# An attentional factorization machine on one core: two fills read from the given table, transposes four rounds later

## The chip, the cores and the metric

The kernel runs on one core of one Trainium2 chip. The metric is the device time of one execution in microseconds. Three executions of the kernel before took 846.13, 851.7 and 852.37 us, median 851.7.

## The reference

For 2048 samples with 32 fields each, rows of an embedding table (12500 x 64) are gathered; only the core of it is shown:

```python
V = emb_v[x]                                     # 32 x 2048 x 64
iu, ju = np.triu_indices(32, k=1)                # 496 pairs of fields
VV = V[iu] * V[ju]
hid = relu(einsum('pbk,kh->pbh', VV, at_w) + at_b)   # 64 -> 64
score = einsum('pbh,ho->pbo', hid, at_h)
pooled = sum(VV * score, axis=0)
logit = pooled @ p + w0 + sum(w1[x], axis=0)     # w1: 12500 x 1
prob = sigmoid(logit)
```

All of it is float32. `x` is drawn below 100000, and the reference clamps it to the table.

## The kernel before, in words

**Fills.** The batch is cut into 32 fills (`FILLS`) of 64 samples, 16 from each quarter of the batch, in two groups g of 32. A fill needs 16 indirect gathers of 128 rows each (line 276): tile (g, m) and half, into one of two buffers `rows[t % 2]`. TensorE transposes the gathered rows (`turn`, eight 128x128 transposes) into a slot of the PSUM buffer `Z`; ScalarE copies them to `V` (`keep_v`, line 424).

**The joint table.** The linear weight `w1[x]` is needed beside the embedding. So the head of the kernel loads the whole table in four pieces and a tail of 212 rows, joins it with `w1` into rows of 66 numbers (w1, embedding, w1; lines 327 to 332 on VectorE, 454 on ScalarE), and stores them as `table` in DRAM (`store_piece`, SP lines 243 to 246 and ScalarE line 456). From then on a gather brings 65 numbers from `table` with `joint_idx`. Only the first group of fill 0 is gathered from the given `emb_v`, and its w1 values are gathered at the end (line 302, 8 gathers). GpSimd waits for `table_stored` before the second group of fill 0.

**Rounds.** A fill has 16 rounds, (step s, group g). VectorE makes the products of pairs `X` (line 409, two instructions a round, four step slots), TensorE multiplies by `at_w` (`hidden`, line 549, into one of three `Z` slots), ScalarE applies bias and ReLU (line 489, into `H`), and TensorE reduces by `at_h` (`scores`, line 564), two steps at a time: after round 3 those of steps 6 and 7 of the fill before, after rounds 7, 11 and 15 those of steps 0 to 5 (`SCORED_AFTER`). I call hidden rounds h0 to h15 and the four score blocks s67, s01, s23, s45.

**Grams.** The pooled sum is taken through the pairwise products weighted by p: ScalarE makes two halves of `pV` (`keep_pv`, line 435), TensorE multiplies `pV` by `V` (`grams`, line 579, 128 small matmuls into `SG`), VectorE masks them (`mask_gram`, line 370), and once all eight steps are scored it multiplies and sums (`weigh` line 378, `sum_pairs` line 384). `grams(t)` must be masked before the first score of fill t is added to the same PSUM tile.

**Order.** Each engine's order is written out by hand; fill 0 is written separately, then a loop with two fills a turn (`over_fills`), then the last fill. In the kernel before, the transposes of fill t+1 are put before h8 of fill t (`TURN_BEFORE = 8`), `keep_v` in ScalarE's round 8, the halves of `pV` in rounds 10 and 14, `keep_w1` (copy of the w1 columns, line 443) in round 12, and the grams of fill t+1 after s45 of fill t. VectorE masks at round 8, weighs at 10, sums at 12. GpSimd's gathers of fill t are paced in four groups of four by the `scored` and `z_ready` counts of fills t-3 and t-2 (`GROUP_AFTER`).

**Head and end.** SP issues the index loads, two table pieces, the tail and nine small loads; ScalarE two pieces and w1. TensorE begins with `first_turn(0)` only after `consts_ready` and all nine small loads, then `keep_busy`, h0 to h3 of group 0, `first_turn(1)`, and the rest. At the end `linear_term` (line 622) waits for the late w1 gathers.

## Time and profile before

| | us |
|---|---|
| median of three executions | 851.7 (846.13 to 852.37) |
| the profiled execution | 846.66 |
| its span | 844.6 |
| TensorE matmul busy | 785.1 (93%) |
| VectorE busy | 701.3 (83%) |
| ScalarE busy | 648.1 (77%) |
| GpSimd busy | 549.0 (65%) |
| mean granted TensorE clock | 0.988 |

The span is the profiled execution from its first to its last instruction; 2.1 us lie around it. In the page a time behind a bar, "idle before", is what the engine stood still ahead of these instructions. In a timeline the bracket at the end of a row gives that idle time and who ended it. "issue" is a wait for which the profile shows no other engine. SPq and ACTq are the DMA issues of SyncE and ScalarE.

### The profile page before, as it was taken

What the parts mean: (1) busy time and instruction counts of PE and PEld (TensorE: products, weight loads), DVE (VectorE), ACT (ScalarE), POOL (GpSimd) and SP (SyncE); (2) the same over time, 40 slices, a digit from 0 to 9 for tenths busy, and PEclk for the clock granted to TensorE, in tenths of its full rate; (3) what the DMA queues carried; (4) which work ended last, traced back from release to release, by engine and by line L of the source; (5) the groups of instructions that cost most, each with busy time, mean ns of one, the idle gap of its engine ahead of it and who ended that gap; (6) DMA issues with size and microseconds to landing.
All of it is one profiled execution on the core that took longest, in us unless ns stands there. A gap on an engine that the chain in (4) does not pass through costs nothing.

```text
span 844.6 us, 30455 instructions
## 1 busy us (share of the span) xinstructions
PE 785.1 (93%) x12600; PEld 336.8 (40%) x12600; DVE 701.3 (83%) x1181; ACT 648.1 (77%) x679; POOL 549.0 (65%) x530
## 2 busy tenths in 40 slices
PE   0368799999999999999999999999999999999998
PEld 0123344444434444444344444434444444344443
DVE  3367788889988888899888889998888899888883
ACT  2256577878888788888878888887878788887885
POOL 4377776666677666666776666667766666767500
PEclk9979899999999999999999999999999999999999
DMA  7458887532424436333233436352322436323100
GB/s 238 107 26 26 25 25 26 22 22 22 22 23 23 21 21 23 21 22 23 22 23 22 22 21 22 22 25 20 23 22 21 22 21 23 24 20 23 9 1 2
DMA packets 19138, 24.20 MB, mean 29 GB/s; under 512 B 9705, under 2 KB 9774, under 8 KB 19118
## 3 DMA queue, kind: packets, MB, share of 16 engines
q0 software_dynamic: 16640, 17.07, 39.5%
q1 hardware_dynamic: 1703, 3.61, 1.1%
q10 hardware_dynamic: 774, 3.25, 1.0%
q8 instruction: 13, 0.21, 0.1%
q14 instruction: 8, 0.06, 0.0%
HBM read 20.59 MB, written 3.31 MB: 28 GB/s over the span
## 4 chain that ended last, share of the span: by engine, by line
PE 83%; POOL 4%; issue 4%; DVE 3%; DMA 3%; SPq 2%; ACT 0%; DVEq 0%; POOLq 0%
PE Z L549 50%; PE SG L564 26%; POOL rows L276 4%; PE SG L579 4%; PE Z L513 4%; DVE X L409 3%; DMA table<-joined 1%; DMA rows<-table,joint_idx 1%; SPq L236 1%; PE Z L634 0%; SPq L237 0%; SPq L229 0%; SPq L239 0%; SPq L238 0%; DVE part L384 0%
## 5 line engine op out<-in xcount | busy, mean ns | idle before, releaser
L276 POOL DMA_INDIRECT rows<-table,joint_idx x504 | 531.0, 1054 | 233.9 <-issue 144.9
L409 DVE TENSOR_TENSOR X<-V 128x992 f32<-128x992 f32 (+15 forms) x1024 | 635.9, 692 | 40.9 <-PE Z L549 22.0
L489 ACT ACTIVATE H<-Z,bias 128x1024 f32<-128x1024 f32 x512 | 536.6, 1118 | 112.5 <-PE Z L549 109.2
L549 PE MATMUL Z<-X,w_sb 64*64 64x512 f32 x4096 | 473.6, 598 | 9.2 <-issue 5.1
L549 PEld LDWEIGHTS Z<-X,w_sb 64*64 64x64 f32 x4096 | 153.0, 133 | 242.4 <-issue 237.4
L564 PE MATMUL SG<-H,score_w 128*32 128x496 f32 (+15 forms) x4096 | 248.4, 382 | 0.0
L564 PEld LDWEIGHTS SG<-H,score_w 128*32 128x32 f32 x4096 | 109.4, 110 | 204.0 <-issue 109.5
L435 ACT ACTIVATE pV<-V,pmask 128x1024 f32<-128x1024 f32 x64 | 81.0, 1269 | 0.1
L378 DVE TENSOR_TENSOR prod<-SG,gram 128x496 f32<-128x496 f32 x32 | 21.6, 674 | 67.5 <-PE SG L564 67.5
L424 ACT COPY V<-Z 128x1024 f32<-128x1024 f32 x31 | 31.4, 1014 | 43.0 <-PE Z L513 43.0
L579 PE MATMUL SG<-V,pV 128*32 128x32 f32 x4096 | 43.7, 198 | 3.2 <-ACT pV L435 1.6
L579 PEld LDWEIGHTS SG<-V,pV 128*32 128x32 f32 x4096 | 43.1, 109 | 7.1 <-issue 3.8
L513 PE MATMUL Z<-ident,rows 128*128 128x128 f32 x248 | 34.7, 284 | 5.8 <-DMA rows<-table,joint_idx 5.8
L525 PE MATMUL SG<-ident,rows 128*128 128x128 f32 x8 | 2.2, 428 | 38.7 <-DMA rows<-in_L_rec_emb_v_dram,idx 29.9
L513 PEld LDWEIGHTS Z<-ident,rows 128*128 128x128 f32 x248 | 27.3, 143 | 8.7 <-DMA rows<-table,joint_idx 5.0
L370 DVE TENSOR_TENSOR gram<-SG,upper 128x496 f32<-128x496 f32 x32 | 21.6, 675 | 9.8 <-PE SG L579 8.2
L384 DVE TENSOR_REDUCE part<-prod 128x496 f32 (+1 forms) x32 | 21.1, 660 | 0.0
L525 PEld LDWEIGHTS SG<-ident,rows 128*128 128x128 f32 x8 | 1.4, 216 | 39.5 <-issue 29.9
L276 POOL DMA_INDIRECT rows<-in_L_rec_emb_v_dram,idx x8 | 9.3, 1168 | 10.4 <-DVE idx L317 8.3
L358 DVE COPY score_w<-hcol 64x1 f32<-64x1 f32 x32 | 2.2, 150 | 10.3 <-DMA w_sb<-in_L_rec_w_dram 10.3
L443 ACT COPY w_all<-rows 128x8 f32 (+2 forms) x64 | 10.4, 227 | 0.0
L463 ACT COPY V<-SG 128x512 f32<-128x512 f32 x2 | 1.2, 587 | 12.1 <-PE SG L525 12.1
(42 smaller groups left out, 31.9 us busy)
## 6 DMA issues: line engine op xcount, KB each, us to landing
rows<-table,joint_idx POOLq DMA_INDIRECT x504, 3.7
table<-joined ACTq DMA_DIRECT2D x2, 792.0 KB
table<-joined SPq DMA_DIRECT2D x2, 792.0 KB
raw<-in_L_rec_emb_v_dram ACTq DMA_DIRECT2D x2, 768.0 KB, 6.7
raw<-in_L_rec_emb_v_dram SPq DMA_DIRECT2D x2, 768.0 KB, 9.1
idx_raw<-in_r_x_dram SPq DMA_DIRECT2D x4, 64.0 KB, 5.9
rows<-in_L_rec_emb_v_dram,idx POOLq DMA_INDIRECT x8, 6.6
w_all<-in_L_rec_w_dram,idx POOLq DMA_INDIRECT x8
```

The source lines that it names most:

```text
L276: pool.indirect_dma_start(out=rows[t % 2][:, g * FILL_M + m, half, c0:c1], out_offset=None, in_=source, in_offset=bass.IndirectOffsetOnAxi ...
L370: nc.vector.tensor_tensor(gram[parity][:, :, 1:FIELDS], SG[parity][:, :, 1:FIELDS], upper[:, 1:FIELDS].unsqueeze(1).to_broadcast(shape), A ...
L378: nc.vector.tensor_tensor(prod[:, :, 1:FIELDS], SG[parity][:, :, 1:FIELDS], gram[parity][:, :, 1:FIELDS], ALU.mult).then_inc(prod_ready, 1)
L384: nc.vector.tensor_reduce(part[:, bass.ds(t * GROUP, GROUP)], prod[:, :, 1:FIELDS], AX.X, ALU.add).then_inc(part_ready, 1)
L409: last_one = nc.vector.tensor_tensor(xo, vj, vi.unsqueeze(3).to_broadcast(shape), ALU.mult)
L424: nc.scalar.copy(V[parity][:, :, :], Z[:, TURN_SLOT, :, :].rearrange("p g (b f) -> p (g b) f", f=FIELDS)).then_inc(v_ready, 1)
L435: nc.scalar.activation(pV[:, :, half, :, :], V[parity][:, :, :].rearrange("p b (i c) -> p b c i", c=2), ACT.Copy, scale=pmask[:, half:half ...
L489: nc.scalar.activation(H[:, s % H_SLOTS, :, COLS * g:COLS * g + COLS], Z[:, z_slot(r), :, :], ACT.Relu, bias=bias[:, 0:1]).then_inc(hid_re ...
L513: last = nc.tensor.transpose(Z[:, TURN_SLOT, g, 128 * m:128 * m + 128], embs[:, g * FILL_M + m, 1:1 + 2 * EMB], ident[:, :])
L549: done = nc.tensor.matmul(Z[64 * par:64 * par + 64, z_slot(r), half, :], w_sb[k, :], X[k, s % X_SLOTS, par, COLS * g:COLS * g + COLS], sta ...
L564: last = nc.tensor.matmul(SG[parity][at:at + 32, :, j0:FIELDS], score_w[:, slot, :], hid.rearrange("p (b j) -> p b j", j=nj), start=(s == ...
L579: last = nc.tensor.matmul(SG[parity][at:at + 32, b, :], pV[:, g * GROUP + b, half, :, :].rearrange("p c i -> p (c i)"), V[parity][:, g * G ...
```

## The change

1. Fills 0 and 1 (`PLAIN_FILLS = 2`) are gathered wholly from `emb_v` with the plain indices; the 32 w1 gathers that replace their w1 columns come at the end. `keep_w1` of fills 0 and 1 and the two memsets of the w1 columns go.
2. All four joined pieces and the tail are stored by SP, after the 16 gathers of fill 0 have landed. GpSimd waits for the table only before fill 2.
3. The index loads are split, two on SP and two on ScalarE's queue, where they are first; w1 comes ahead of the pieces there, w1's tail moves to SP, and its join (two copies) from VectorE to ScalarE.
4. `first_turn(0)` comes before the wait for the constants, and `keep_busy` makes four matmuls instead of eight.
5. The transposes of fill t+1 move from before h8 to before h12, with `keep_v`; `keep_w1` to round 14; the halves of `pV(t)` to rounds 0 and 2 of fill t itself, and the grams of fill t behind s67, after h3 of fill t. VectorE masks at 10, weighs at 11, sums at 13. The transposes of fill 1 keep their own slot.
6. The gathers of fill t are paced later: from two more scored steps (line 267) and from z_ready 6, 10 and 13 instead of 3, 7 and 10.

The declarations of two semaphores are left out below.

```diff
--- before.py
+++ after.py
@@ -43,7 +43,9 @@
 ORDER = [(s, g) for s in range(STEPS) for g in range(2)]
 FIRST_ORDER = [(s, g) for g in range(2) for s in range(STEPS // 2)] + ORDER[ROUNDS // 2:]
 
-TURN_BEFORE = 8
+TURN_BEFORE = 12
+PV_BEFORE = (0, 2)
+MASKED_BEFORE, WEIGHED_BEFORE, SUMMED_BEFORE = 10, 11, 13
 SCORED_AFTER = {3: (-1, (6, 7)), 7: (0, (0, 1)), 11: (0, (2, 3)), 15: (0, (4, 5))}
 LAST_STEPS = (6, 7)
 
@@ -55,9 +57,10 @@
 PIECES = 4
 PIECE = RUN // PIECES
 MAIN = 128 * RUN
+PLAIN_FILLS = 2
 TAIL_RUN = 4
 TAIL = (VOCAB - MAIN) // TAIL_RUN
-GROUP_AFTER = (0, 3, 7, 10)
+GROUP_AFTER = (0, 6, 10, 13)
 
 
 def segments(s):
@@ -71,7 +74,7 @@
     return (r if r < TURN_BEFORE else r + 1) % Z_SLOTS
 
 
-TURN_SLOT = TURN_BEFORE % Z_SLOTS
+TURN_SLOT, FIRST_TURN_SLOT = TURN_BEFORE % Z_SLOTS, Z_SLOTS - 1
 
 
 def z_before(r):
@@ -222,28 +225,33 @@
         def store_piece(eng, k):
             eng.dma_start(piece(table, k), joined[:, k * PIECE:(k + 1) * PIECE, :]).then_inc(table_stored, 16)
 
+        def load_idx(eng, q):
+            eng.dma_start(idx_raw[q * FIELDS:(q + 1) * FIELDS, :], r_x[:, q * NB:(q + 1) * NB]).then_inc(idx_loaded, 16)
+
         @block.sync
         def _(sp):
 
-            for q in range(QUARTERS):
-                sp.dma_start(idx_raw[q * FIELDS:(q + 1) * FIELDS, :],
-                             r_x[:, q * NB:(q + 1) * NB]).then_inc(idx_loaded, 16)
+            for q in range(QUARTERS // 2):
+                load_idx(sp, q)
             for k in range(PIECES // 2):
                 load_piece(sp, k)
             sp.dma_start(tail[:, :, 1:1 + EMB], last_rows(emb_v)).then_inc(tail_loaded, 16)
+            sp.dma_start(tail_w1[:, :], w1[MAIN:VOCAB, :].rearrange("(p r) o -> p (r o)", r=TAIL_RUN)).then_inc(tail_loaded, 16)
             for half in range(2):
                 lo, hi = half * 64, half * 64 + 64
-                sp.dma_start(pcol[lo:hi, :], p).then_inc(small_loaded, 16)
+                sp.dma_start(w_sb[lo:hi, :], at_w).then_inc(small_loaded, 16)
                 sp.dma_start(bias[lo:hi, :], at_b.rearrange("(h o) -> h o", o=1)).then_inc(small_loaded, 16)
                 sp.dma_start(hcol[lo:hi, :], at_h).then_inc(small_loaded, 16)
-                sp.dma_start(w_sb[lo:hi, :], at_w).then_inc(small_loaded, 16)
+                sp.dma_start(pcol[lo:hi, :], p).then_inc(small_loaded, 16)
             sp.dma_start(w0_sb[:, :], w0.to_broadcast([QUARTERS, 1])).then_inc(small_loaded, 16)
-            sp.wait_ge(w1_joined, 4)
-            sp.wait_ge(tail_loaded, 16)
-            sp.dma_start(last_rows(table), tail[:, :, :]).then_inc(table_stored, 16)
-            for k in range(PIECES // 2):
+            for g in range(2):
+                sp.wait_ge(first_rows[g], 16 * GATHERS // 2)
+            sp.wait_ge(w1_joined, 2)
+            for k in range(PIECES):
                 sp.wait_ge(rows_joined[k], 1)
                 store_piece(sp, k)
+            sp.wait_ge(tail_joined, 2)
+            sp.dma_start(last_rows(table), tail[:, :, :]).then_inc(table_stored, 16)
             sp.wait_ge(y_ready, 1)
             sp.dma_start(out.rearrange("(q a m) o -> a q (m o)", q=QUARTERS, a=QUARTERS), y_sb[:, :, :]).then_inc(y_stored, 16)
             sp.wait_ge(y_stored, 16)
@@ -259,16 +267,16 @@
 
             flat = table.rearrange("v (k o) -> (v k) o", o=1)
 
-            def gather(t, groups=(0, 1), paced=False):
-
-                for g in groups:
+            def gather(t, paced=False):
+
+                joint = t >= PLAIN_FILLS
+                source, at_rows = (flat, joint_idx) if joint else (emb_v, idx)
+                for g in range(2):
                     for m in range(FILL_M):
                         if paced and g == 0 and m == 0:
-                            pool.wait_ge(scored, STEPS * (t - 3) + LAST_STEPS[0] - 1)
+                            pool.wait_ge(scored, STEPS * (t - 3) + LAST_STEPS[0] + 1)
                         elif paced and m % 2 == 0:
                             pool.wait_ge(z_ready, ROUNDS * (t - 2) + GROUP_AFTER[2 * g + m // 2])
-                        joint = t > 0 or g > 0
-                        source, at_rows = (flat, joint_idx) if joint else (emb_v, idx)
                         for half in range(2):
                             col = (2 * half + g) * NM + t * FILL_M + m
                             c0, c1 = (0, ROW) if joint else (EMB_AT[half], EMB_AT[half] + EMB)
@@ -278,28 +286,24 @@
                                                     in_offset=bass.IndirectOffsetOnAxis(ap=at_rows[:, col:col + 1], axis=0)
                                                     ).then_inc(arrived, 16)
 
-            for half in range(2):
-                nc.gpsimd.memset(rows[0][:, 0:FILL_M, half, W1_AT[half]], 0.0).then_inc(w1_cleared, 1)
             pool.wait_ge(idx_ready, 1)
-            gather(0, groups=(0,))
+            gather(0)
+            pool.wait_ge(idx_ready, 2)
+            gather(1)
             pool.wait_ge(idx_ready, 4)
             pool.wait_ge(table_stored, 16 * (PIECES + 1))
-            gather(0, groups=(1,))
-            gather(1)
             pool.wait_ge(first_turned, 2)
-            pool.wait_ge(w1_kept, 2)
             gather(2)
             pool.wait_ge(rows_turned, 1)
-            pool.wait_ge(w1_kept, 4)
             gather(3)
             for t in range(4, FILLS):
                 pool.wait_ge(rows_turned, t - 2)
-                pool.wait_ge(w1_kept, 2 * (t - 1))
+                pool.wait_ge(w1_kept, 2 * (t - 3))
                 gather(t, paced=True)
-            for half in range(2):
-                for n in range(FILL_M):
-                    at = bass.IndirectOffsetOnAxis(ap=idx[:, 2 * half * NM + n:2 * half * NM + n + 1], axis=0)
-                    pool.indirect_dma_start(out=w1_all[:, 2 * half, n:n + 1], out_offset=None, in_=w1, in_offset=at
+            for Q in range(QUARTERS):
+                for n in range(PLAIN_FILLS * FILL_M):
+                    at = bass.IndirectOffsetOnAxis(ap=idx[:, Q * NM + n:Q * NM + n + 1], axis=0)
+                    pool.indirect_dma_start(out=w1_all[:, Q, n:n + 1], out_offset=None, in_=w1, in_offset=at
                                             ).then_inc(w1_first, 16)
 
         @block.vector
@@ -322,10 +326,9 @@
                                         ).then_inc(idx_ready, 1)
 
 
-            dve.wait_ge(w1_loaded, 32)
+            dve.wait_ge(w1_loaded, 16)
             for c in (0, 1 + EMB):
                 nc.vector.tensor_copy(joined[:, :, c], raw_w1[:, :]).then_inc(w1_joined, 1)
-                nc.vector.tensor_copy(tail[:, :, c], tail_w1[:, :]).then_inc(w1_joined, 1)
             for k in range(PIECES // 2):
                 dve.wait_ge(raw_loaded[k], 16)
                 r0, r1 = k * PIECE, (k + 1) * PIECE
@@ -390,11 +393,11 @@
                 for r, (s, g) in enumerate(FIRST_ORDER if first else ORDER):
                     if first and r in (0, STEPS // 2):
                         dve.wait_ge(first_v, g + 1)
-                    if r == 8:
+                    if r == MASKED_BEFORE:
                         mask_gram(t, parity)
-                    if r == 10 and not first:
+                    if r == WEIGHED_BEFORE and not first:
                         weigh(t - 1, 1 - parity)
-                    if r == 12 and not first:
+                    if r == SUMMED_BEFORE and not first:
                         sum_pairs(t - 1)
                     if not first:
                         dve.wait_ge(z_ready, ROUNDS * t + r - 2 * X_SLOTS + 1)
@@ -421,7 +424,8 @@
                 if not (isinstance(t, int) and t == 1):
                     act.wait_ge(x_ready, ROUNDS * (t - 1))
                     act.wait_ge(gram_ready, t - 1)
-                nc.scalar.copy(V[parity][:, :, :], Z[:, TURN_SLOT, :, :].rearrange("p g (b f) -> p (g b) f", f=FIELDS)
+                slot = FIRST_TURN_SLOT if isinstance(t, int) and t == 1 else TURN_SLOT
+                nc.scalar.copy(V[parity][:, :, :], Z[:, slot, :, :].rearrange("p g (b f) -> p (g b) f", f=FIELDS)
                                ).then_inc(v_ready, 1)
 
             def keep_pv(t, parity, half):
@@ -437,25 +441,24 @@
 
             def keep_w1(t, parity):
 
-                g0 = 1 if isinstance(t, int) and t == 0 else 0
                 for half in range(2):
-                    src = rows[parity][:, :, half, W1_AT[half]].rearrange("p (g m) -> p g m", g=2)[:, g0:2, :]
-                    nc.scalar.copy(w1_all[:, 2 * half + g0:2 * half + 2, bass.ds(t * FILL_M, FILL_M)], src
+                    src = rows[parity][:, :, half, W1_AT[half]].rearrange("p (g m) -> p g m", g=2)
+                    nc.scalar.copy(w1_all[:, 2 * half:2 * half + 2, bass.ds(t * FILL_M, FILL_M)], src
                                    ).then_inc(w1_kept, 1)
 
+            for q in range(QUARTERS // 2, QUARTERS):
+                load_idx(nc.scalar, q)
+            nc.scalar.dma_start(raw_w1[:, :], w1[0:MAIN, :].rearrange("(p r) o -> p (r o)", p=128)).then_inc(w1_loaded, 16)
             for k in range(PIECES // 2, PIECES):
                 load_piece(nc.scalar, k)
-            nc.scalar.dma_start(raw_w1[:, :], w1[0:MAIN, :].rearrange("(p r) o -> p (r o)", p=128)).then_inc(w1_loaded, 16)
-            nc.scalar.dma_start(tail_w1[:, :], w1[MAIN:VOCAB, :].rearrange("(p r) o -> p (r o)", r=TAIL_RUN)).then_inc(w1_loaded, 16)
-            act.wait_ge(w1_joined, 3)
             for k in range(PIECES // 2, PIECES):
                 act.wait_ge(raw_loaded[k], 16)
                 r0, r1 = k * PIECE, (k + 1) * PIECE
                 nc.scalar.copy(joined[:, r0:r1, 1:1 + EMB], raw[:, r0:r1, :]).then_inc(rows_joined[k], 1)
-                act.wait_ge(rows_joined[k], 1)
-                store_piece(nc.scalar, k)
+            act.wait_ge(tail_loaded, 32)
+            for c in (0, 1 + EMB):
+                nc.scalar.copy(tail[:, :, c], tail_w1[:, :]).then_inc(tail_joined, 1)
             act.wait_ge(small_loaded, 16 * 9)
-            act.wait_ge(w1_cleared, 2)
             nc.scalar.activation(warm[:, :], w0_sb[:, :], ACT.Sigmoid).then_inc(sigmoid_loaded, 1)
             def first_keep_v(g):
 
@@ -467,19 +470,16 @@
             def relus(t, parity, first, last):
                 for r in range(ROUNDS):
                     if not last and not first:
-                        if r == 8:
+                        if r == TURN_BEFORE:
                             keep_v(t + 1, 1 - parity)
-                        if r == 10:
-                            keep_pv(t + 1, 1 - parity, 0)
-                        if r == 12:
+                        if r == 14:
                             keep_w1(t + 1, 1 - parity)
-                        if r == 14:
-                            keep_pv(t + 1, 1 - parity, 1)
+                    if not first and r in PV_BEFORE:
+                        keep_pv(t, parity, PV_BEFORE.index(r))
                     if first and r == STEPS // 2:
                         first_keep_v(1)
                         for half in range(2):
                             keep_pv(0, 0, half)
-                        keep_w1(0, 0)
 
                     act.wait_ge(z_ready, ROUNDS * t + r + 1)
 
@@ -490,9 +490,6 @@
                                          bias=bias[:, 0:1]).then_inc(hid_ready, 1)
                 if first:
                     keep_v(1, 1)
-                    for half in range(2):
-                        keep_pv(1, 1, half)
-                    keep_w1(1, 1)
 
             over_fills(act, relus)
             act.wait_ge(logit_ready, 1)
@@ -507,10 +504,11 @@
                     pe.wait_ge(second_rows, 16 * GATHERS)
                 else:
                     pe.wait_ge(rows_gathered[parity], gathered(t, parity))
+                slot = FIRST_TURN_SLOT if isinstance(t, int) and t == 1 else TURN_SLOT
                 embs = rows[parity][:, :, :, :].rearrange("p t h k -> p t (h k)")
                 for g in range(2):
                     for m in range(FILL_M):
-                        last = nc.tensor.transpose(Z[:, TURN_SLOT, g, 128 * m:128 * m + 128],
+                        last = nc.tensor.transpose(Z[:, slot, g, 128 * m:128 * m + 128],
                                                    embs[:, g * FILL_M + m, 1:1 + 2 * EMB], ident[:, :])
                 last.then_inc(rows_turned, 1)
 
@@ -583,10 +581,10 @@
                 last.then_inc(gram_ready, 1)
 
             pe.wait_ge(ident_ready, 1)
+            first_turn(0)
             pe.wait_ge(consts_ready, 1)
             pe.wait_ge(small_loaded, 16 * 9)
-            first_turn(0)
-            keep_busy(8)
+            keep_busy(4)
 
             def products(t, parity, first, last):
                 for r in range(ROUNDS):
@@ -608,13 +606,13 @@
                                 scores(t, parity, s)
                             elif not first:
                                 scores(t - 1, 1 - parity, s)
-                    if r == ROUNDS - 1 and not last:
-                        grams(t + 1, 1 - parity)
+                        if back < 0 and not first:
+                            grams(t, parity)
 
             def linear_term():
 
-                pe.wait_ge(w1_first, 16 * 2 * FILL_M)
-                pe.wait_ge(w1_kept, 2 * FILLS)
+                pe.wait_ge(w1_first, 16 * QUARTERS * PLAIN_FILLS * FILL_M)
+                pe.wait_ge(w1_kept, 2 * (FILLS - PLAIN_FILLS))
                 pe.wait_ge(hid_ready, ROUNDS * FILLS)
                 for Q in range(QUARTERS):
                     for q in range(QUARTERS):
```

## Rows read from the trace of the kernel before

**Rows 1.** The page: granted TensorE clock in tenths, 40 slices of 21.1 us.

```profile
...
PEclk9979899999999999999999999999999999999999
...
```

**Rows 2.** Timeline of the first 80 us: start us, us, instruction [idle before <-releaser].

```profile
...
4.77 8.67 SPq L236 DMA_DIRECT2D pcol<-in_L_rec_p_dram  x1
...
9.16 0.17 DVE L313 TENSOR_SCALAR gram<-idx_raw 128x16 f32<-128x16 int32 x1 [9.16 <-DMA idx_raw<-in_r_x_dram]
...
10.04 1.11 POOL L276 DMA_INDIRECT rows<-in_L_rec_emb_v_dram,idx  x1 [8.28 <-DVE idx L317]
...
19.25 0.66 SPq L240 DMA_DIRECT2D w_sb<-in_L_rec_w_dram  x1
...
20.57 0.95 POOL L276 DMA_INDIRECT rows<-in_L_rec_emb_v_dram,idx  x1 [0.30 <-issue]
...
27.49 2.17 DVE L358 COPY score_w<-hcol 64x1 f32<-64x1 f32 x32 [10.31 <-DMA w_sb<-in_L_rec_w_dram]
...
33.65 4.16 PE L549 MATMUL Z<-X,w_sb 64*64 64x512 f32 x32
...
46.56 1.11 PE L525 MATMUL SG<-ident,rows 128*128 128x128 f32 x4 [8.76 <-DMA rows<-table,joint_idx]
...
56.01 9.99 DVE L409 TENSOR_TENSOR X<-V 128x736 f32<-128x736 f32 x16
...
69.16 1.07 PE L513 MATMUL Z<-ident,rows 128*128 128x128 f32 x8 [0.96 <-DMA rows<-table,joint_idx]
...
```

**Rows 3.** The chain that ended last, 15 to 100 us: start us, us, what.

```profile
...
20.81 11.90 DMA table<-joined
...
83.92 9.37 DMA rows<-table,joint_idx
...
```

**Rows 4.** The page: groups (busy, mean ns | idle), DMA issues (us to landing).

```profile
...
L276 POOL DMA_INDIRECT rows<-table,joint_idx x504 | 531.0, 1054 | 233.9 <-issue 144.9
L409 DVE TENSOR_TENSOR X<-V 128x992 f32<-128x992 f32 (+15 forms) x1024 | 635.9, 692 | 40.9 <-PE Z L549 22.0
...
L564 PE MATMUL SG<-H,score_w 128*32 128x496 f32 (+15 forms) x4096 | 248.4, 382 | 0.0
...
rows<-table,joint_idx POOLq DMA_INDIRECT x504, 3.7
...
rows<-in_L_rec_emb_v_dram,idx POOLq DMA_INDIRECT x8, 6.6
...
```

**Rows 5.** TensorE's timeline from 76 to 180 us, columns as in rows 2.

```profile
...
93.34 1.97 PE L513 MATMUL Z<-ident,rows 128*128 128x128 f32 x8 [4.86 <-DMA rows<-table,joint_idx]
...
109.65 3.66 PE L549 MATMUL Z<-X,w_sb 64*64 64x512 f32 x32
...
132.43 1.30 PE L579 MATMUL SG<-V,pV 128*32 128x32 f32 x128
134.19 3.66 PE L549 MATMUL Z<-X,w_sb 64*64 64x512 f32 x32 [0.47 <-issue]
...
158.32 3.66 PE L549 MATMUL Z<-X,w_sb 64*64 64x512 f32 x32
...
```

**Rows 6.** Waits from 100 to 800 us: waiter <- releaser: us, times, longest.

```profile
...
DVE prod L378 <- PE SG L564: 55.8, 29, 2.0
...
PE Z L549 <- issue: 5.1, 12, 0.5
...
```

**Rows 7.** ScalarE's timeline from 130 to 186 us, columns as in rows 2.

```profile
...
146.27 1.01 ACT L424 COPY V<-Z 128x1024 f32<-128x1024 f32 x1 [1.16 <-PE Z L513]
147.40 2.12 ACT L489 ACTIVATE H<-Z,bias 128x1024 f32<-128x1024 f32 x2
149.41 1.27 ACT L435 ACTIVATE pV<-V,pmask 128x1024 f32<-128x1024 f32 x1
...
```

**Rows 8.** TensorE's timeline from 740 us on, columns as in rows 2.

```profile
...
838.92 1.05 PE L622 MATMUL Z<-w_all,pick 32*4 32x128 f32 x32
...
```

**Rows 9.** The instructions of line 302: ns min/median/max, first and last start us.

```profile
...
L302 POOL DMA_INDIRECT w_all<-in_L_rec_w_dram,idx x8: 947/948/1023, 786.7 to 795.6; - x8
...
```

4 lines of the change are left out of this document (2 added, 2 removed).

## The prediction, made before the changed kernel was run

> **What bounds the kernel now.** I read the waits first, then the timeline of the head, then the chain, and last one fill of the steady part.
>
> From 100 to 800 us TensorE waits for almost nothing: 5.1 us in 12 gaps before h0, none of them for rows or products [rows 6]. Two fills take 48.67 us (h0 at 109.65, 134.19 and 158.32: 24.54 and 24.13) [rows 5], so 24.3 us each. The longer one holds the loop's jump back, with a gap of 0.47 us after the grams [rows 5]. VectorE needs 635.9/32 = 19.9 us of products a fill [rows 4], some 21.9 with mask, weighing and sum (0.67 each): it has 2.4 us spare, and shows it by waiting 1.9 us a fill for the scores at `weigh` [rows 6]. So the steady part is TensorE's own work.
>
> The head is not. The first index is seen at 9.16, the first gather starts at 10.04, h0 starts at 33.65, since the constants come at 27.49 + 2.17 [rows 2]. Then TensorE stands 8.76 us before the second half's transposes at 46.56 [rows 2], since these rows come from the joint table, whose storing ends the chain's 11.90 us piece at 32.7 [rows 3]. Fill 1's rows make it wait 0.96 us more (69.16) [rows 2], fill 2's 4.86 us (93.34) [rows 5]; the last gather of fill 2 took 9.37 us to land [rows 3], against a median of 3.7 [rows 4]. The clock is below 9 tenths in the third and fifth slice (7 and 8) [rows 1]: after these stands some work ran at the lower level. The eight transposes of fill 2 took 1.97 us behind their stand of 4.86, those of fill 1 1.07 [rows 5, 2].
>
> So I ask two things: when does h0 of fill 2 start (109.65 before), and does the steady 24.3 us survive the new order.
>
> **The head, step by step.**
>
> (a) Indices. The four loads of 64 KB stood behind 1.5 MB of ScalarE's pieces; now they are first on both queues. They need no more than the 5.9 us that they took, less what the pieces cost them. Bounds: 4.5 us (hardly above the 3.7 us in which gathers land [rows 4]) and 9.16 as now [rows 2]. I take 5.0, so the first gather starts at 5.9 (10.04 − 9.16 = 0.88 behind [rows 2]). I lean to the low end because only the order in the queues kept them back. The Trainium skill (DMA: Bandwidth & Descriptors, Rules for kernel authors) says that spreading DMAs over SP and ScalarE saves issue time only, since all run on the same 16 engines. By it the indices would come hardly sooner, and the sum below would come out 3 us later.
>
> (b) Fill 0's rows. Eight gathers took 10.04 to 20.57, 1.50 us apart with one long one; undisturbed they are 0.95 + 0.30 = 1.25 apart [rows 2]. Sixteen: 5.9 + 15 x 1.25 + 1.5 for a long one = 26.2 for the last start. Landing 3.7 to 6.6 us [rows 4]: 30 to 33.
>
> (c) Constants. SP stood 8.67 us in one small issue at 4.77, until its pieces had gone, and ended its last at 19.9 [rows 2]; with one more issue, 20.5. That one landed only by 27.49, with the stores around it. The stores are gone from there: 3.7 us [rows 4] instead of 7.6 gives 24.2; +2.17 for the copies, +0.3, +1.24 for one round of products: h0 at 27.9, before 33.65. Bounds for the landing are 2 and 7.6 us: h0 at 26 to 32. The transposes of group 0 and half of `keep_busy` are hidden under this. h0 to h3 take 4.16 [rows 2]: end 32.1, and the second half's rows are there. `first_turn(1)` at **32** against 46.56.
>
> (d) From there to the turn of fill 1: before 69.16 − 46.56 = 22.6 [rows 2], with grams and rounds at the low clock and 0.96 of waiting. Without a stand of 8.76 us I take the high clock: 1.1 + 0.6 + 2.5 + 0.9 to the end of h5, grams 1.3 [rows 5], ten rounds of 0.9, two score blocks of 1.94 (248.4/128 [rows 4]): 19.3 us. TensorE is there at 51.3.
>
> (e) Fill 1's rows. Last gather: 26.2 + 16 x 1.25 + 0.5 = 46.7. Behind the stores, which go out from 32 on. Landing 3.7 to 9.4 us [rows 4, 3], I take 6.6, the value of gathers among stores and loads [rows 4]: 53.3. Turn of fill 1 at **53.3**, a stand of 2 us (bounds 51.3 and 56; a longer stand would also bring some low clock, as behind 88.5).
>
> (f) To the turn of fill 2, now before h12. After a turn: 1.1 + 1.0 for V, 1.24 for products, four rounds at VectorE's 1.24 and 0.9 after the last: 8.1; s67 1.9; grams 1.35; then h4 to h7, s01, h8 to h11, s23, 3.6 + 1.9 + 3.6 + 1.9: **22.3** in all, 75.6. The two instructions of `keep_pv` (1.27 [rows 7]) no longer stand before h0, since grams(1) now comes behind s67.
>
> (g) Fill 2's rows. GpSimd is free at 48. The stores, issued from 32.5 on, took from 14.9 to 32.7 before on two queues, the last 11.9 us after their issue [rows 3]: 12 to 18 us give 45 to 50.5, I take 48.5. What waits behind SP's new wait for fill 0's rows is the stores alone, and behind them GpSimd's gathers of fill 2 on. Sixteen gathers take 20.5 us: 69, landing 3.7 to 9.4: 72.7 to 78.4, I take 76. Turn of fill 2 at **76**. Later by four rounds than the old place, this turn forgives 5.5 us of lateness.
>
> (h) h0 of fill 2: turn 1.0, four rounds 3.6, s45 1.9: **82.5** against 109.65. Before, the grams of fill 2 were done by then, now they follow: +1.35. Net **−25.8 us**.
>
> **The steady part.** The counts of instructions are the same, but for two `keep_w1` pairs, so nothing is gained or lost but by waits. Times here are from the start of a turn. V is copied from 1.13 to 2.14 (146.27 lies 1.13 behind its turn [rows 7]). VectorE, which stands for V up to 2.4 us, has X of round 0 at 3.4, and h0 is due at 6.5: 3 us spare; at h3 (7.2 against 9.2) 2 us. VectorE no longer waits 1.9 us for scores, it waits as long for V. Mask: VectorE reaches round 10 some 8 us into the fill, the grams end 6.9 us into it, s01 is due at 10.5, the mask takes 0.7: 1.6 us spare. ScalarE: relu 12 and 13 at 2.3 and 3.3, w1 copies 0.3, relu 14 and 15 end at 5.6 and 6.7 (a relu each 1.0 [rows 7]), due 6.5 and 7.4. Then pV 1.17, relu 0 from 7.8 to 8.9, and h3 needs it at 9.2: **0.3 us spare**, the tightest place. The second pV ends at 11.1, grams are due at 12.0. Gathers: sixteen at 1.054 + 0.30 [rows 4] = 21.7 us, below 24.3; they start 4.6 us into a fill and end at 26.5, rows due 15 us later. So 0. The loop's gap of 0.47 now lies behind s45, whose instructions are longer than the grams' 10 ns, so part of 15 x 0.4 = 6 us may hide; the other end is ScalarE's own jump in front of pV, of like size. I take 0, bounds −6 and +6.
>
> **The end.** 32 late w1 gathers instead of 8. From h0 of fill 29, 79.6 us before the end, GpSimd needs 26.6 for fill 31's gathers and 32 x 1.27 (8.9/7 [rows 9]) = 40.6; with 3.7 to land that is 8.7 us before the end. The linear term is due 5.7 before it (838.92 [rows 8]). 3 us spare: 0, at worst 3 late.
>
> **Sum.** 846.66 − 25.8 = 820.9 for the profiled execution. It lies 5.0 below the median 851.7. On the median: 851.7 − 25.8 = 825.9, and I say **825**.
>
> **The rivals.**
>
> *The wait moves to the table (12 in 100).* The stores now start at 32, not 15. If single-queue stores and gathers hinder each other as they did from 15 to 33, the table is there at 53 or later, fill 2's rows land at 53 + 20.5 + 9.4 = 83, and late rows bring a low clock again (+2). For: 9.37 us landing [rows 3]. Against: half as many packets of loads beside them. Gain 26 − 9 = 17 us: 835; with fill 1's rows late too, 841.
>
> *The indices gain nothing (15 in 100, part of the forecast's 70).* If all transfers of the first 10 us share the engines evenly, whatever their order, the first gather starts near 10.04 as before [rows 2], the last of fill 0 at 30.3, its rows land at 34 to 37, `first_turn(1)` comes at 35 and all behind it 3 us later: 829. This is how the skill's rule named in (a) would come out here.
>
> *Head gained, steady part gives back half (7 in 100).* If h3 waits 0.4 to 0.6 us for relu 0 in each of 31 fills, +12 to +19: 838 to 845, near no change.
>
> *Slower: pV on the path (4 in 100).* Before, the two pV lay in ScalarE's spare time behind a turn. Now they stand right at the edge of a fill, where relu 0 and relu 1 feed h3 and h4. If ScalarE runs 0.3 us late, each further tenth is TensorE's. It decides at 25.8/31 = 0.83 us a fill; with one pV of 1.17 wholly in TensorE's way, 851.7 − 25.8 + 31 x 1.17 = 862. Against: the count above has it there in time, and the second pV has relu 2 behind it, which h5 needs only 2 us after it is done.
>
> *More (6 in 100).* Constants at 26, no stand at either turn, the loop gap hidden: −25.8 − 2 − 3 − 5 = 816 on the median, 811 with the low execution.
>
> *The change does not do what it says*: if the first rows of `emb_v` came no sooner, T would stay at 46; nothing points to it, 1 in 100.
>
> **How the numbers follow.** Forecast 70 in 100 for 817 to 833. The range 812 to 838 takes in the first rival's nearer half and the gains; 2 in 10 are outside. A difference below 1%, 8.5 us, is what a measurement of this kernel cannot tell from none. Faster by over 1% (below 843.2): 0.90; same 0.06; slower by over 1% 0.04.
>
> **What would show it.** First plain gather near 6 us, h0 near 28, `first_turn(1)` near 32 with no stand before it, turn of fill 1 near 53, of fill 2 near 76, h0 of fill 2 near 82.5, and 24.3 us a fill after. Wrong would be: the table stored after 50, a wait for relu 0 before h3 in each fill, or the linear term waiting for w1.

## The result: 1.2% slower, and the profile after

Thirteen executions of the changed kernel have a median of 861.62 us (855.37 to 866.98), thirteen of the kernel before beside it 852.28 us (843.28 to 854.0). The ratio is 1.0123, with a 95% interval of 1.0097 to 1.015. The forecast was 825 (812 to 838), with 4 in 100 for slower: it is wrong in its sign. The profiled execution of the kernel before is one of its quick ones (846.66 against a median of 852.28), so the two traces lie 14.4 us apart where the medians lie 9.3 apart.

The profiled execution took 860.83 us, its span is 859.0 against 844.6, 14.4 us more. The clock is no part of it (0.99 in both). Three markers split the span:

| | before | after | difference |
|---|---|---|---|
| start to h0 of fill 2 | 109.65 | 96.56 | −13.1 |
| from there to the end of the scores | 729.3 | 746.3 | +17.1 |
| from there to the end | 5.7 | 16.1 | +10.4 |

So the start up to this marker gained half of the 27.2 us that were forecast for it, and the two other parts, forecast at nothing but the 1.35 us of fill 2's grams, cost 27.5 us.

**The head.** The timeline of the kernel after (start us, us, instruction, idle before and its releaser), to be read beside [rows 2]:

```profile
...
3.62 0.17 DVE L317 TENSOR_SCALAR gram<-idx_raw 128x16 f32<-128x16 int32 x1 [3.62 <-DMA idx_raw<-in_r_x_dram]
...
4.50 1.11 POOL L284 DMA_INDIRECT rows<-in_L_rec_emb_v_dram,idx  x1 [2.83 <-DVE idx L321]
...
21.38 0.65 SPq L246 DMA_DIRECT2D w_sb<-in_L_rec_w_dram  x1
...
30.14 2.17 DVE L361 COPY score_w<-hcol 64x1 f32<-64x1 f32 x32 [15.45 <-DMA w_sb<-in_L_rec_w_dram]
...
34.19 5.20 PE L547 MATMUL Z<-X,w_sb 64*64 64x512 f32 x32
...
35.99 3.11 SPq L226 DMA_DIRECT2D table<-joined  x4
...
39.32 0.66 PE L523 MATMUL SG<-ident,rows 128*128 128x128 f32 x4
...
54.49 2.02 PE L562 MATMUL SG<-H,score_w 128*32 128x16 f32 x19 [3.81 <-issue]
...
65.74 0.94 POOL L284 DMA_INDIRECT rows<-table,joint_idx  x1 [19.70 <-issue]
...
```

The first gather starts at 4.50 instead of 10.04, the stand of 8.76 us before the second half's transposes is gone (39.32 instead of 46.56). But the last small load, issued at 21.38, is seen only at 30.14, and GpSimd stands for 19.70 us until the table is there at 65.7. In this kernel the chain that ended last runs through that small load: SP's issues up to 21.38, its 8.74 us to land, the constants, h0, and from there TensorE's own pace to the turn of fill 2.

**The steady part.** TensorE's timeline after, from 90 us on, to be read beside [rows 5]:

```profile
...
90.08 1.09 PE L511 MATMUL Z<-ident,rows 128*128 128x128 f32 x8
...
96.56 3.66 PE L547 MATMUL Z<-X,w_sb 64*64 64x512 f32 x32
...
117.00 1.06 PE L511 MATMUL Z<-ident,rows 128*128 128x128 f32 x8 [1.48 <-DMA rows<-table,joint_idx]
...
128.80 2.06 PE L577 MATMUL SG<-V,pV 128*32 128x32 f32 x128
130.81 3.66 PE L547 MATMUL Z<-X,w_sb 64*64 64x512 f32 x32
...
155.59 3.66 PE L547 MATMUL Z<-X,w_sb 64*64 64x512 f32 x32
...
```

Between 130.81 and 155.59 lie 24.78 us; a fill took 24.3 before. Every line of it has the length that it had, but one: the grams take 2.06 us, where they took 1.30 [rows 5]. The loop's gap of 0.47 is gone, 0.24 a fill; so +0.76 − 0.24 = +0.5 a fill, and TensorE waits for nobody. From the turn of fill 3 to that of fill 31 the mean of a fill is 24.79 us, before 24.34: times 29 that is 13 of the 17.1 us. The grams of fill 2, done before the marker in the kernel before, add 2.04, and the turn of fill 3 waits 1.48. The two pages show where the grams lose (after, then before; busy us, mean ns of one):

```profile
...
L577 PE MATMUL SG<-V,pV 128*32 128x32 f32 x4096 | 61.2, 201 | 4.8 <-issue 0.3
...
```

```profile
...
L579 PE MATMUL SG<-V,pV 128*32 128x32 f32 x4096 | 43.7, 198 | 3.2 <-ACT pV L435 1.6
...
```

One matmul is as long as it was, 201 ns against 198; they follow each other at a greater distance (1.30 and 2.06 us over 128 are 10 and 16 ns), and the whole run's grams take 17.5 us more.

Who shares the time of the grams? GpSimd's timeline of the kernel after:

```profile
...
153.93 0.94 POOL L284 DMA_INDIRECT rows<-table,joint_idx  x1 [0.30 <-PE SG L562]
...
162.40 3.88 POOL L284 DMA_INDIRECT rows<-table,joint_idx  x1 [0.30 <-issue]
...
178.71 0.95 POOL L284 DMA_INDIRECT rows<-table,joint_idx  x1 [0.30 <-PE SG L562]
...
```

and of the kernel before, where the grams of [rows 5] start at 132.43:

```profile
...
132.56 1.80 POOL L276 DMA_INDIRECT rows<-table,joint_idx  x1 [3.02 <-PE SG L564]
...
```

Before, GpSimd had finished its sixteen gathers with time over and paused 3.02 us at the pacing wait for the scores; the next gather started 0.13 us behind the grams and was itself stretched to 1.80 (what held it is told with VectorE's moves below). After, it never pauses: but for some gaps as long as one gather, at which the trace shows no wait for another engine, every gather follows the last by the bare 0.30 us. A fill's first gather starts at 153.93 and the next fill's at 178.71, so GpSimd needs the whole 24.78 us, and in nearly every fill one gather takes 3.9 us (26 over 3 us in the run, two of them late w1 gathers; none before). In the page the gathers' mean rose from 1054 ns [rows 4] to 1204:

```profile
...
L284 POOL DMA_INDIRECT rows<-table,joint_idx x480 | 578.0, 1204 | 177.7 <-issue 168.9
...
```

The waits of the whole run (waiter <- releaser: us, times, longest) say the same, and where it ends:

```profile
...
PE Z L620 <- DMA w_all<-in_L_rec_w_dram,idx: 9.6, 1, 9.6
...
POOL rows L284 <- PE SG L562: 8.5, 28, 0.3
...
PE Z L547 <- ACT H L489: 0.2, 1, 0.2
...
```

GpSimd's 28 waits for the scores are 0.3 us each, its bare step (before 72.6 us in 27). TensorE waits 0.2 us for a relu in the whole run. And line 620, the linear term, waits 9.6 us for w1: this is the end's +10.4, the rest of it being the lower clock behind that stand (granted 0.50 of full speed from 850 to 855 us), 1.89 us instead of 1.05 for its 32 products.

### The profile page after: what moved, and what is told of

Read it like the earlier page. It is cut to its first block, busy times and chain, and to the rows that moved or that the text cites. A ratio compares the mean times of both kernels' runs of the same rounds, so it can differ in the third digit from the quotient of the medians.

```text
span 859.0 us, 30478 instructions
## 1 busy us (share of the span) xinstructions
PE 800.8 (93%) x12596; PEld 345.0 (40%) x12596; DVE 695.1 (81%) x1179; ACT 647.8 (75%) x677; POOL 649.8 (76%) x552
## 4 chain that ended last, share of the span: by engine, by line
PE 83%; POOL 8%; issue 3%; SPq 2%; DMA 2%; ACT 1%; DVE 0%; POOLq 0%; DVEq 0%; ACTq 0%
PE Z L547 48%; PE SG L562 25%; PE SG L577 6%; POOL w_all L306 4%; POOL rows L284 3%; PE Z L511 3%; SPq L239 1%; DMA w_sb<-in_L_rec_w_dram 1%; ACT H L489 1%; DMA rows<-table,joint_idx 1%; SPq L242 0%; DMA w_all<-in_L_rec_w_dram,idx 0%; DVE score_w L361 0%; PE Z L632 0%; PE SG L531 0%
## 5 line engine op out<-in xcount | busy, mean ns | idle before, releaser
L284 POOL DMA_INDIRECT rows<-table,joint_idx x480 | 578.0, 1204 | 177.7 <-issue 168.9
L547 PEld LDWEIGHTS Z<-X,w_sb 64*64 64x64 f32 x4096 | 150.7, 133 | 232.1 <-issue 224.7
L577 PE MATMUL SG<-V,pV 128*32 128x32 f32 x4096 | 61.2, 201 | 4.8 <-issue 0.3
L577 PEld LDWEIGHTS SG<-V,pV 128*32 128x32 f32 x4096 | 54.2, 110 | 18.4 <-issue 13.2
L306 POOL DMA_INDIRECT w_all<-in_L_rec_w_dram,idx x32 | 38.8, 1213 | 9.8 <-issue 9.8
L284 POOL DMA_INDIRECT rows<-in_L_rec_emb_v_dram,idx x32 | 32.1, 1003 | 12.3 <-issue 9.1
L511 PEld LDWEIGHTS Z<-ident,rows 128*128 128x128 f32 x248 | 26.5, 141 | 7.6 <-issue 4.1
L381 DVE TENSOR_TENSOR prod<-SG,gram 128x496 f32<-128x496 f32 x32 | 21.1, 661 | 8.5 <-PE SG L562 8.5
L373 DVE TENSOR_TENSOR gram<-SG,upper 128x496 f32<-128x496 f32 x32 | 21.1, 661 | 0.0
```

Source lines behind the costliest of these rows:

```text
L284: pool.indirect_dma_start(out=rows[t % 2][:, g * FILL_M + m, half, c0:c1], out_offset=None, in_=source, in_offset=bass.IndirectOffsetOnAxi ...
L306: pool.indirect_dma_start(out=w1_all[:, Q, n:n + 1], out_offset=None, in_=w1, in_offset=at).then_inc(w1_first, 16)
L373: nc.vector.tensor_tensor(gram[parity][:, :, 1:FIELDS], SG[parity][:, :, 1:FIELDS], upper[:, 1:FIELDS].unsqueeze(1).to_broadcast(shape), A ...
L381: nc.vector.tensor_tensor(prod[:, :, 1:FIELDS], SG[parity][:, :, 1:FIELDS], gram[parity][:, :, 1:FIELDS], ALU.mult).then_inc(prod_ready, 1)
L511: last = nc.tensor.transpose(Z[:, slot, g, 128 * m:128 * m + 128], embs[:, g * FILL_M + m, 1:1 + 2 * EMB], ident[:, :])
L547: done = nc.tensor.matmul(Z[64 * par:64 * par + 64, z_slot(r), half, :], w_sb[k, :], X[k, s % X_SLOTS, par, COLS * g:COLS * g + COLS], sta ...
```

## The experiments

**Theory G**: GpSimd no longer pauses over the grams, and gathers running beside them hold up their short matmuls. **Theory O**: their place behind s67 costs the 0.7 us, whatever GpSimd does. **Theory L**: GpSimd's own work, lengthened by a gather of 3.9 us, fills the whole fill and delays the end.

The first four kernels ran first in a job in which the kernel before itself takes 1224 us (in its trace of gathers over grams TensorE stands on its own issue for some 190 us). Their ratios to before there (old pacing 1.0269, head alone 1.023, order alone 0.9753, gathers over grams 0.9865) say nothing of 1% here. The same four were run again in an ordinary job, before at 852.71 us, and are told from there.

### Old pacing

```diff
-GROUP_AFTER = (0, 6, 10, 13)
+GROUP_AFTER = (0, 3, 7, 10)
...
-                            pool.wait_ge(scored, STEPS * (t - 3) + LAST_STEPS[0] + 1)
+                            pool.wait_ge(scored, STEPS * (t - 3) + LAST_STEPS[0] - 1)
```

> The changed kernel with only the pacing of the gathers put back (first wait two scored steps earlier, z_ready 0, 3, 7, 10). Theory G (a running gather of GpSimd stops TensorE's issue for 0.28 us about twice in 1.25 us, which the short grams cannot hide): gathers start 5.5 us earlier in a fill but still run over h0 to h7 and the grams, so these stay at 2.05 us and a fill at 24.8 us; the late w1 gathers end 5 to 10 us earlier, so the wait of 9.6 us before the linear term goes; span 848 to 852, from 859.0. Theory P (the later pacing is what costs in each fill): grams back at 1.30, a fill at 24.3, span about 835. Theory O (their place behind s67 makes the grams slow, whatever GpSimd does): as G.

858.93 us (855.25 to 867.41), ratio 1.0087 (1.0048 to 1.0126), the span 854.8. Grams 2.03, 24 gathers over 3 us, and the linear term still waits 8.35 us. The forecast had this wait gone and the span at 848 to 852. So the later pacing is not what lost the time: GpSimd is late by its own work, and an earlier permission is of little use to it. In one fill the trace has no gather from 746.35 to 752.40, and TensorE's timeline has there:

```profile
...
746.34 1.30 PE L577 MATMUL SG<-V,pV 128*32 128x32 f32 x128
...
770.37 2.03 PE L577 MATMUL SG<-V,pV 128*32 128x32 f32 x128
...
```

From 746.34 to 770.37 are 24.03 us: in this one fill the new order with 1.30 us of grams is faster than the old 24.3.

### The head alone (parts 1 to 4 of the change, old order and pacing)

```diff
-TURN_BEFORE = 12
+TURN_BEFORE = 8
...
-MASKED_BEFORE, WEIGHED_BEFORE, SUMMED_BEFORE = 10, 11, 13
+MASKED_BEFORE, WEIGHED_BEFORE, SUMMED_BEFORE = 8, 10, 12
...
+                    if r == ROUNDS - 1 and not last:
+                        grams(t + 1, 1 - parity)
```

> The head of the changed kernel (parts 1 to 4) with the order and the pacing of the kernel before. Theories G, P and O agree on the steady part: grams 1.30 us, 24.3 us a fill. If the head's gain of 13 us holds without the later turn, the span is 830 to 834; if fill 2's rows, due 5.5 us earlier in this order, are late, TensorE waits up to 6 us for them and it is 836 to 840. The linear term should not wait for w1 by more than 2 us.

844.98 us (843.29 to 846.18), ratio 0.9927 (0.9899 to 0.9954): faster. TensorE's timeline:

```profile
...
90.44 1.97 PE L515 MATMUL Z<-ident,rows 128*128 128x128 f32 x8 [7.38 <-DMA rows<-table,joint_idx]
...
153.87 1.31 PE L581 MATMUL SG<-V,pV 128*32 128x32 f32 x128
...
```

Grams at 1.31, no gather over 3 us, and the 32 w1 gathers of the end cost nothing: the linear term has no wait. At the old place the turn of fill 2 waits 7.38 us for the late table. The forecast spans (830 to 834, or 836 to 840 with late rows) were missed: 842.3, only 2.3 under the trace of before, with h0 of fill 2 at 106.02 instead of 109.65. The rest of the 0.7% in the medians is that the kernel before is mostly slower than its profiled execution, for which no trace here gives a reason.

### The order and the pacing alone (parts 5 and 6 on the kernel before)

```diff
-TURN_BEFORE = 8
+TURN_BEFORE = 12
+PV_BEFORE = (0, 2)
+MASKED_BEFORE, WEIGHED_BEFORE, SUMMED_BEFORE = 10, 11, 13
...
-GROUP_AFTER = (0, 3, 7, 10)
+GROUP_AFTER = (0, 6, 10, 13)
```

> The kernel before with parts 5 and 6 alone (transposes before h12, grams behind s67, later pacing), its own head and eight late w1 gathers. Theories G and O: grams 2.05 us, a fill 24.8 us, +0.47 x 29 = 14 us, less up to 5 us of the wait for fill 2's rows, which the later turn forgives: span 850 to 858 against 844.6. Had the order been free, as the prediction said, 838 to 843.

851.62 us (849.32 to 858.03), ratio 1.0022 (0.9988 to 1.0056). TensorE's timeline:

```profile
...
94.24 1.09 PE L513 MATMUL Z<-ident,rows 128*128 128x128 f32 x8
...
100.72 3.66 PE L549 MATMUL Z<-X,w_sb 64*64 64x512 f32 x32
...
131.71 2.05 PE L579 MATMUL SG<-V,pV 128*32 128x32 f32 x128
...
```

The turn of fill 2 no longer waits (4.86 before), h0 of fill 2 is 8.9 us earlier, and the steady part gives all of it back and more: 743.1 us from there to the end of the scores instead of 729.3 (2.1 of it the grams of fill 2), with grams at 2.05 and 23 long gathers. The span is 849.5, just under the forecast 850 to 858. With 8 w1 gathers the linear term has no wait.

So the steady loss belongs to the order, and the wait at the end to both halves together: 0.9927 x 1.0022 = 0.995, while both with old pacing gave 1.0087. The missing 1.4% are some 12 us; 8.35 of them are the wait for the w1 gathers.

### Gathers over the grams, in the kernel before

```diff
-                            pool.wait_ge(scored, STEPS * (t - 3) + LAST_STEPS[0] - 1)
+                            pool.wait_ge(scored, STEPS * (t - 3) + LAST_STEPS[0] - 4)
```

> The kernel before with one number changed: the first pacing wait is three scored steps earlier, so that GpSimd no longer pauses ahead of the grams and gathers 5 to 8 of a fill run over them. Theory G: grams 1.8 to 2.1 us instead of 1.30, a fill 24.7 to 25.0 us, span 855 to 862. Theory O: nothing changes, 843 to 846, since the grams stay behind s45.

869.28 us (863.77 to 872.94), ratio 1.0222 (1.0162 to 1.0281). Nothing but one constant of one wait of GpSimd is changed; the grams are at their old place. The timeline, at two grams:

```profile
...
132.35 1.29 PEld L579 LDWEIGHTS SG<-V,pV 128*32 128x32 f32 x100
132.39 0.95 POOL L276 DMA_INDIRECT rows<-table,joint_idx  x1 [0.31 <-issue]
132.49 2.10 PE L579 MATMUL SG<-V,pV 128*32 128x32 f32 x128
133.64 0.94 POOL L276 DMA_INDIRECT rows<-table,joint_idx  x1 [0.30 <-issue]
133.81 0.27 PEld L579 LDWEIGHTS SG<-V,pV 128*32 128x32 f32 x19 [0.18 <-issue]
...
232.85 1.34 PEld L579 LDWEIGHTS SG<-V,pV 128*32 128x32 f32 x128
233.00 1.30 PE L579 MATMUL SG<-V,pV 128*32 128x32 f32 x128
...
234.48 0.94 POOL L276 DMA_INDIRECT rows<-table,joint_idx  x1 [3.16 <-issue]
...
```

With gathers in a row the grams take 2.10 us, their weight loads broken by idle stretches; in the fill where GpSimd stood for 3.16 us they take 1.30, in one unbroken run of 128. The span is 861.6, as theory G had it (855 to 862). Theory G stands, theory O falls. GpSimd was not short of time here: it waits 94.4 us in all for z_ready. What counts is where it runs, not how much.

Two readings narrow what "beside them" means. It is not the gathers' transfers: during the grams at 132.43 in the kernel before the gathers' queue holds 47.5% of the DMA engines' time, and the grams take 1.30; during those at 153.58 in the kernel after it holds 45.0%, and they take 2.06. And it is not a gather that stands: one gather of this run lasts from 369.84 to 384.61, and the grams at 382.81, wholly inside it, take 1.30.

### The gathers held for the grams, in the kernel after

```diff
-                            pool.wait_ge(scored, STEPS * (t - 3) + LAST_STEPS[0] + 1)
+                            pool.wait_ge(gram_ready, t - 1)
```

> The changed kernel with one wait exchanged: the first gather of fill t waits until the grams of fill t-2 are done, instead of for a scored step, so that GpSimd stands while the grams run. Theory G: grams back at 1.30 us where GpSimd has come to the wait before them, a fill at 24.0 to 24.1 us (the loop's gap hidden), span 835 to 842, with the wait for the late w1 gathers still there or longer. If GpSimd itself needs more than a fill's time in this order (theory L: a gather that meets VectorE's unbroken last rounds takes 3.9 us), it comes too late for the wait, grams stay at 2.05 in most fills, and the span is 855 to 862. Theory O: grams at 2.05 everywhere, 859.

862.15 us (861.67 to 862.52), ratio 1.0119 (1.0068 to 1.0171). In all but five fills GpSimd comes to the wait when it is long fulfilled; grams 2.05 in nearly all fills (1.30 in three), 24 gathers over 3 us, and the linear term waits 12.06 us. A wait can't put the pause back where there is no time for one: theory L.

### Weigh at round 12 and the sum at 14, in the kernel after

```diff
-MASKED_BEFORE, WEIGHED_BEFORE, SUMMED_BEFORE = 10, 11, 13
+MASKED_BEFORE, WEIGHED_BEFORE, SUMMED_BEFORE = 10, 12, 14
```

> The changed kernel with VectorE's weighing before round 12 instead of 11 and the sum before 14 instead of 13; nothing else. Theory L (the 3.9 us gather is one that meets VectorE's unbroken rounds 13 to 15): it stays, since VectorE still runs without a break up to its wait for V, 3.5 to 3.9 us once a fill, and the span stays at 855 to 862. If it hangs on the sum ahead of round 13, the long gather goes, GpSimd needs 22 us a fill, pauses, and grams fall to 1.3 us in part of the fills: span 835 to 850.

848.01 us (844.12 to 852.22), ratio 0.9959 (0.9926 to 0.9993), where the kernel after has 1.0123: some 14 us off it by moving two instructions of VectorE one round each. A wait of GpSimd, and then its timeline:

```profile
...
POOL rows L284 <- PE SG L562: 40.0, 28, 3.9
...
```

```profile
...
135.24 3.37 POOL L284 DMA_INDIRECT rows<-table,joint_idx  x1 [3.85 <-PE SG L562]
138.91 2.69 POOL L284 DMA_INDIRECT rows<-table,joint_idx  x1 [0.30 <-issue]
141.91 2.68 POOL L284 DMA_INDIRECT rows<-table,joint_idx  x1 [0.30 <-issue]
...
```

GpSimd pauses again, the gathers over 3 us fell from 26 to 9, and the linear term waits for nothing. In about every third fill, as here, the grams take 1.3 us; but in such a fill four gathers in a row take 2.7 to 3.4 us, GpSimd falls behind, and in the next two fills the grams are back at 2.05. Where the gain of the profiled execution lies is plain from TensorE's turn of fill 31: it starts at 810.95, in the kernel after at 810.97. The grams' 6 us were lost again ahead of it, to a wait of 3.92 for fill 2's rows, a stand of 2.83 within its grams and lower clock behind both. All of its 10.4 us lie at the end, in the w1 gathers that are no longer late.

**What a long gather waits for.** VectorE's timeline of the kernel after, to be read beside the gather of 3.88 us at 162.40:

```profile
...
161.78 3.69 DVE L412 TENSOR_TENSOR X<-V 128x608 f32<-128x608 f32 x6
...
```

and VectorE's and GpSimd's of *gathers over the grams*:

```profile
...
369.20 14.59 DVE L409 TENSOR_TENSOR X<-V 128x608 f32<-128x608 f32 x24
...
369.84 14.77 POOL L276 DMA_INDIRECT rows<-table,joint_idx  x1 [0.30 <-issue]
...
```

The first gather ends at 166.28, 0.81 us behind the end of VectorE's unbroken series of products; the second at 384.61, 0.82 behind its series of 24. It is so for every gather over 2.3 us from 100 us on, 132 in six runs (this one, the kernel after, old pacing, order alone, gathers over grams, gathers held): each ends 0.81 to 0.83 us behind such a series, wherever in it the gather began. In the rows above 138.61, 141.60 and 144.59 are the ends, and mask, weighing and sum break VectorE's products at 137.79, 140.77 and 143.76. The 1.80 us of the kernel before ends in the same way. So a long gather is one that is held until VectorE's products break, and it is as long as the series that it meets. And a held gather leaves the grams alone (1.30 to 1.32 at all eight such places of this run). What decides which gather is held was not found: in the kernel after, between 100 and 800 us, 280 gathers began in a series that had over 1.6 us to go, and 23 of them were held to its end.

### The nine small loads first, on the head alone

```diff
-            for k in range(PIECES // 2):
-                load_piece(sp, k)
...
             sp.dma_start(w0_sb[:, :], w0.to_broadcast([QUARTERS, 1])).then_inc(small_loaded, 16)
+            for k in range(PIECES // 2):
+                load_piece(sp, k)
```

> The head of the changed kernel with the old order and pacing (842.3 span when run before), and the nine small loads moved ahead of SP's table pieces. Theory A (in this head the chain runs through the stores of the table and the gathers of fill 2, not through the constants): h0 starts at 26 to 29 instead of 37.5, first_turn(1) at 34 to 37 instead of 42.1, but the wait for fill 2's rows grows from 7.4 to 12 us or more and the span falls by under 2 us: 840 to 843. Theory C (constants are on the chain): 5 to 9 us less, 834 to 837.

844.33 us (843.4 to 853.58), ratio 0.9934 (0.9898 to 0.9971), as the head alone. TensorE's timeline:

```profile
...
33.86 6.22 PE L551 MATMUL Z<-X,w_sb 64*64 64x512 f32 x32 [5.94 <-DVE X L412]
...
91.03 1.97 PE L515 MATMUL Z<-ident,rows 128*128 128x128 f32 x8 [4.97 <-DMA rows<-table,joint_idx]
...
```

h0 starts at 33.86 instead of 37.47, not at 26 to 29 as expected, since it now waits 5.94 us for VectorE's products. By the turn of fill 1 the gain is gone, 66.73 against 63.65: TensorE stands 3.98 us on its own issue, where it stood 0.17, and behind that stand its next block takes 5.45 us instead of 3.66. Fill 2's turn, which waits for the table's rows in both, is no earlier, 91.03 against 90.44. So with the old order the table bounds the head. For the kernel after this does not follow: its later turn of fill 2 had no wait, and these loads were not moved there.

### The stores at once, on the head alone

```diff
-            for g in range(2):
-                sp.wait_ge(first_rows[g], 16 * GATHERS // 2)
```

> The head of the changed kernel with the old order and pacing, and SP's stores of the table no longer held back until fill 0's rows have landed. Theory A: the table is there at 35 to 45 instead of 64, the gathers of fill 2 start when those of fill 1 are issued, at 47, and TensorE does not wait for them (7.4 us before), or little; fill 0's rows land 5 to 8 us later, which costs part of it again; span 836 to 840. Theory S (holding the stores back is right): first_turn(1) slips by more than is gained, 843 to 848.

843.06 us (840.31 to 848.59), ratio 0.9904 (0.9876 to 0.9933): the fastest kernel of this study, 1.0% under the kernel before, though its interval overlaps that of the head alone (0.9899 to 0.9954). SyncE's, GpSimd's and TensorE's rows of its timeline:

```profile
...
20.00 2.94 SPq L226 DMA_DIRECT2D table<-joined  x4
...
63.28 0.94 POOL L282 DMA_INDIRECT rows<-table,joint_idx  x1 [16.92 <-issue]
...
87.52 1.09 PE L513 MATMUL Z<-ident,rows 128*128 128x128 f32 x8 [0.56 <-DMA rows<-table,joint_idx]
...
```

The stores are issued 16 us sooner than in the head alone (36.07), and GpSimd's first joint gather is only 3.1 us sooner (66.36 there), not 18 as hoped. The DMA queues between 20 and 66 us tell part of why (packets, MB, share of 16 engines' time), first of the kernel after, then of this one:

```profile
...
q0 software_dynamic: 781, 0.79, 57.7%
q1 hardware_dynamic: 1279, 3.33, 18.2%
...
```

```profile
...
q0 software_dynamic: 800, 0.81, 60.2%
q1 hardware_dynamic: 1078, 3.32, 17.9%
...
```

Queue 0 holds the gathers, queue 1 SP's stores. In these 46 us the stores took 8.4 us of the sixteen engines for 3.33 MB, the gathers 26.5 us for 0.79 MB. At 33 KB a gather (128 rows of 64 numbers) that is 1.1 us of all engines for each, near GpSimd's pitch of 1.25. So the 32 plain gathers fill much of the engines' time: all queues together hold 92, 87 and 94% of it in the three stretches of 10 us from 20 to 50 in the kernel after, 98, 96 and 95% here. But the pieces of the table were not what came last here: 3.16 of the 3.32 MB were stored by 50 us. The tail's 53 packets, issued behind them, moved only from 55 us on, 40 of them behind 60. GpSimd waited for these. A tail issued first was not tried.

### Half the gathers, the sum alone, weigh alone, and all together

Six runs came in two jobs in which the kernel before takes 1203 and 1229 us. The number recorded for the chip of one of them is that of the job with 852.71 us above, so it is not shown that the chip makes the difference. One kernel leaves out every second gather of fills 4 to 31 of the kernel after:

```diff
-            return 16 * GATHERS // 2 * (t - parity)
+            return 8 * GATHERS + 4 * GATHERS * (t - parity)
...
-                        for half in range(2):
+                        for half in range(1 if paced else 2):
```

> The kernel after, with every second gather of fills 4 to 31 left out (half the rows keep what an earlier fill put there). Theory G: what the grams lose is the gathers' work beside them, not their place behind s67; with 8 gathers a fill GpSimd has time to pause, and grams with no gather in progress take 1.23 to 1.3 us, those with one 1.6 to 2.05; a fill takes 24.0 to 24.4 us, the linear term has no wait, and the time is 861.6 - 29 x 0.5 - 9.6 = 837 (828 to 846). Theory O (the place behind s67 costs the 0.7 us whatever GpSimd does): every gram set stays at 2.03, a fill at 24.8, and only the end's 9.6 us are gained: 852.

947.04 us (939.95 to 951.24), where the kernel with all gathers and the sum at 14 took 1196.92 in the same job: 224 gathers fewer, 250 us less, 1.1 us each (in an earlier job 955.52 and 1198.08). TensorE's and GpSimd's rows at two grams:

```profile
...
524.37 1.68 PE L577 MATMUL SG<-V,pV 128*32 128x32 f32 x128
524.50 3.66 POOL L284 DMA_INDIRECT rows<-table,joint_idx  x1 [7.33 <-PE SG L562]
...
919.07 1.30 PE L577 MATMUL SG<-V,pV 128*32 128x32 f32 x128
...
```

The size can't be carried over (the forecast of 828 to 846 was for the ordinary state of 852 us), but the places can: with a gather that starts at the grams they take 1.67 to 1.70 us in nearly every fill, one idle stretch in the weight loads, and in the two last fills, with no gather left, 1.30, at the same place behind s67. (In the ordinary jobs a gather that began 0.13 us behind the grams left them at 1.30 and was itself stretched; here both are.) That is theory G without theory O once more, now in the kernel after.

To find which of VectorE's two moves makes the long gather, each was tried alone (the sum at 14 with weigh at 11; weigh at 12 with the sum at 13).

> The kernel after with only the sum moved from before round 13 to before round 14 (weigh stays before 11). Theory P: GpSimd's gather of 3.9 us comes from the sum placed between rounds 12 and 13; then nearly all of them vanish, GpSimd pauses again, and the time is that of weigh 12 and sum 14, 848 to 853. Theory Q: it comes from weigh standing right behind the mask, and the sum has no part in it: then 20 or more gathers over 3 us stay, and the time is 858 to 863.

> The kernel after with only weigh moved from before round 11 to before round 12 (the sum stays before 13). Theory P (the sum's place makes the long gather): 20 or more gathers over 3 us stay, 858 to 863. Theory Q (weigh's place makes it): fewer than 10 stay, 848 to 853.

The sum alone took 1196.92 us (before 1203.32 in its job) and in the other job 1198.08, weigh alone 1189.11, both against 1229.48. Their traces have 19 and 24 gathers over 3 us with the sum alone, 16 with weigh alone, 7 with both. With a kernel before that is 40% off its time, and the kernel after not run beside them, this does not tell the two apart: it stays open.

> The kernel after with weigh at 12, the sum at 14, and without SP's wait for fill 0's rows before the stores. If the two gains add, the head's 1.9 us (843.06 against 844.98 with the old order) come on top of the 848.0 of weigh 12 and sum 14: 846. It would beat the fastest so far, 843.06, only if the grams also fell from 2.03 to 1.3 us in most fills; I expect 843 to 848.

All together took 1195.49 us in such a job; whether it would be below 843.06 in an ordinary one is open.

## Why the prediction was wrong, by its steps

**Step (a), indices: right, and more than that.** Seen at 3.62 (5.0 taken), the first gather at 4.50 (5.9; lower bound 5.4). The rule of the Trainium skill (DMA: Bandwidth & Descriptors, Rules for kernel authors), that DMAs spread over several engines run on the same 16 DMA engines and save issue time only, would as I applied it have had them near 9.16. The trace does not bear out my use of it; the rule is not refuted, since it speaks of spreading, and here the order in each queue was changed too. Both together were worth 5.5 us; they were not tried apart.

**Step (b): the start right, the landing late.** The last gather of fill 0 starts at 24.98 (26.2), but SP, which waits for its rows, issues the stores only at 35.99; 30 to 33 was said. It took a landing of 3.7 to 6.6 us from the eight gathers of before, and there were up to thirty-two in a row: between 20 and 30 us their queue alone holds 87.6% of the DMA engines' time.

**Step (c), constants: mis-sized.** 3.7 us to land were taken, 8.7 it took (21.38 to 30.14): it landed among the gathers' packets. h0 at 34.19 (27.9; outside the bounds of 26 to 32), `first_turn(1)` at 39.32 (32). In the kernel after these 6 to 7 us lie on the chain to the turn of fill 2. With these loads first in the head alone nothing was gained, but there the table's rows come later than TensorE.

**Steps (d) and (e): the stand of 2 us at the turn of fill 1 did not come**; the turn is at 66.15 (53.3), since h0 was 6 us late, TensorE stood 3.81 us on its own issue within the first score block (up to 54.49), X was late (4.2 us in two waits), and some of it ran at the low clock (granted 0.83 of full speed from 40 to 60 us). The forecast had taken the high clock.

**Step (g), the table: the largest miss of the head, though not alone on its path.** There at 65.7 where 48.5 was taken (45 to 50.5). It priced the stores by what stores had taken before, among eight gathers; there were thirty-two. The rival *the wait moves to the table* had this mechanism and priced it too low, at 53 and later. It did not show as a wait at the turn of fill 2, since TensorE was itself 14 us late there by steps (c) to (e): turn of fill 2 at 90.08 without a stand, fill 3's 1.48.

**Step (f)/(h): right in kind.** The later turn does forgive: with it the turn of fill 2 had no wait (order alone 94.24, the whole change 90.08), at the old place the same head waits 7.38. h0 of fill 2 is at 96.56 (82.5): −13.1 where −27.2 stood ahead of the grams.

**The steady part failed, and with the end it decided the sign.** "The counts of instructions are the same ... so nothing is gained or lost but by waits": the lengths of the blocks were taken as fixed. The grams took 2.06 us instead of 1.30 since gathers run beside them. And the gathers, counted at 1.054 + 0.30 and 21.7 us a fill, took 24.78, since in the new order of VectorE one of them is held for 3.9 us, until the last products of the fill are done; this, by *weigh at 12 and the sum at 14*, hangs on where the two stand. These two are linked: GpSimd without spare time works through the grams. But the second is not needed for the first, for *gathers over the grams* has GpSimd with time to spare and grams at 2.07. What it did in its 2.6 us of spare time, namely stand still over the grams, was in the trace of before (a pause of 3.02 us that ends at the grams), and the forecast read it as slack. The bounds of −6 and +6 covered the loop's gap only; +17.1 came.

The waits that it counted through all held: V, the mask, relu 0 with its 0.3 us spare (0.2 us in the whole run), pV. The rivals *pV on the path* and *steady part gives back half* did not happen by their mechanism; the second named the size nearly right (+12 to +19) for another reason, by luck.

**The end failed by the same number.** "3 us spare" stood on 21.7 us a fill. With 24.8 GpSimd comes to the 32 w1 gathers late, at 802.11, these take 48.3 us and not 40.6 (two of them are held too), and the linear term waits 9.6 us; in the head alone, with GpSimd at its old speed, the same 32 gathers cost nothing.

**The sum**, each ratio times 852 us: the head alone −6.2, order with pacing alone +1.9, all of it +10.5. So the two together cost 14.8 us more than one by one; the end's wait is 9.6 of them, and with the old pacing the whole change stood at +7.4. The other 5 are not accounted for by a run.

## What to carry to other kernels

An engine's idle time can be what keeps another engine's block of short instructions short: before counting it as spare, look which short instructions fall into the pause, and how long they are in the few fills where the pause was missing. When an order is moved, count durations beside the new neighbours, not only waits. Where a gather of GpSimd is long, look where VectorE's unbroken series ends. And price indirect gathers by the time that they hold the DMA engines, not by their bytes.

## What the runs showed of the hardware

- 128 matmuls of 128x32 take 1.30 us with GpSimd still or in a gather that is held, 1.67 to 1.70 with one gather started beside them in the slower jobs, and 2.03 to 2.10 in a stream of gathers (one matmul 198 and 201 ns); longer matmuls (3.66 us for 32 of 512 columns, 1.93 for 32 scores) are the same in all kernels at the full clock.
- A gather's 0.95 us became 1.8 to 14.8 where it was held by VectorE: all 132 over 2.3 us end 0.81 to 0.83 us behind an unbroken series of VectorE's products of two SBUF tiles. Most gathers begun in such a series are not held (257 of 280 in the kernel after); what selects them was not found.
- A gather of 33 KB held the sixteen DMA engines for 1.1 us in the head (26.5 us for 0.79 MB); plain stores moved 3.33 MB in 8.4 us of them.
- In three jobs this kernel took 1.4 times as long (1203 to 1229 us), and there half of the gathers less took off 250 us of 1197. Why was not found.
